# Attention loop of an adaLN network: exponential in two halves, paired table stores, one copy of the operands, a new order of the loads

## The chip, the cores and the metric

One core of a Trainium2 chip runs the whole kernel. The metric is the device time of one execution in microseconds, median of several; lower is better. Five engines with queues of their own work side by side and synchronise by semaphores: TensorE (PE, its weight loads shown as PEld), VectorE (DVE), ScalarE (ACT), GpSimd (POOL) and SyncE (SP), which here issues the DMAs.

## The reference, cut to what matters

The network has two layers; the change is in the attention of the first. That attention has relative positions, 16 heads of 16 channels, 8 sequences of 1024 tokens:

```python
Q = _heads(x @ Wq.T + bq)
K = _heads(x @ Wk.T + bk)
V = _heads(x @ Wv.T + bv)
rel = jnp.arange(t)[None, :] - jnp.arange(t)[:, None]
rel_pos = jnp.clip(rel + ATT_SPAN, 0, 2 * ATT_SPAN - 1)      # ATT_SPAN = 128
scores = jnp.einsum('bhqd,bhkd->bhqk', Q, K) * scale
c2p = jnp.einsum('bhqd,shd->bhqs', Q, pos_key) * scale
c2p = jnp.take_along_axis(c2p, rel_pos[None, None, :, :], axis=-1)
p2c = jnp.einsum('bhkd,shd->bhks', K, pos_query) * scale
p2c = jnp.take_along_axis(p2c, p2c_pos[None, None, :, :], axis=-1)
scores = scores + c2p + jnp.swapaxes(p2c, -1, -2)
probs = jax.nn.softmax(scores, axis=-1)
ctx = jnp.einsum('bhqk,bhkd->bhqd', probs, V)
```

Before it stand a layer norm with modulation and the projections; behind it an output projection, a quantised feed-forward layer, a second layer with a state-space scan and one more feed-forward layer. The change touches none of these.

## The kernel before, in words

`attention_loop` goes over 128 heads (8 sequences by 16), two to a turn of its loop (`pair`), and in each head over 8 query tiles of 128 rows, `i` = 0 to 7. `m` counts tiles over all heads, `n` counts heads.

The position terms differ from key to key only within 128 positions. For every tile two **tables** of 128 by 384 are computed (queries against relative keys, `e` even, and keys against relative queries, `e` odd), 16 to a head, one head ahead. PE multiplies them into `e_ps` (`table`, L883), ACT copies each to `tab` (`keep_table`, L966), SP stores it to DRAM (`store_table`, L784), and SP reads it back **skewed**, with a row pitch one element shorter, so that relative positions become key positions (`load_skew`, L793). The skewed reads go in four parts of two tiles (`PARTS`), each of four DMAs. A part's reads wait until its tables' stores have landed.

For query tile m the stages are: PE **scores** (L866, bf16 products of operands in `opnd`) plus transposed additions of the skewed key table (L870), DVE **add** of the skewed query table (L1018) and negated row **maximum** (L1020), ACT **exponential** over all 1024 keys (L971), PE **turn**: eight transposes of the probabilities (L899) in two halves of 512 keys, a copy of each half to `probsT` (first half DVE L1025; second half DVE L1028 in even tiles, ACT `keep_second` L978 in odd ones), and PE **context** (L918). Every fourth tile adds `keep_context` (ACT L985), `sum_lanes` (PE L928) and `normalise` (DVE L1036, L1039).

Each engine runs its work in the written order; iteration i (tile m) is:

- PE: scores(m+1), table 2i, turn(m), table 2i+1, at i = 1 and 5 sum_lanes, context(m-1).
- ACT: keep_table 2i, keep_table 2i+1, exps(m+1), at odd i keep_second(m), at i = 0 and 4 keep_context.
- DVE: add and maximum of m+1, copies of turn(m), at i = 1 and 5 normalise.
- SP, at the head's start: the three operand loads of head n+1 (`load_opnd`, L771), two loads of a second operand copy for the tables of head n+2 (`load_eopnd`, L775; the same first 96 rows of the same DRAM arrays). Then in iteration i the stores of tables 2i and 2i+1; behind those of i = 0 the skewed reads of part 3 (tiles 6 and 7 of head n) and the load of the values; behind i = 2, 4 and 6 the skewed reads of parts 0, 1 and 2 of head n+1.

Waits that bind the engines to each other: scores(m+1) needs exps(m-1) done (two score buffers). The scores of tiles 0, 1, 3 and 5 also wait for the skewed reads of parts 0, 1, 2 and 3. turn(m) needs exps(m), and each of its halves needs the copy of the same half of turn(m-1), since `pT_ps` has one buffer for each half. There is one `e_ps`, so table e+1 needs keep_table e done. These two lines carry most of what follows:

```python
ge(pe, s_exp, m + 1)        # turn, first half: the exponential of this tile
ge(pe, s_p1a, n * HALF + i // 2)   # turn, second half, even i: ACT's copy of the tile before
```

Of the kernel before, what the change touches and what calls it, by code (L numbers as in the profile page):

```python
# [15 lines left out]
P = 128  # L16
# [4 lines left out]
SPAN = 128  # L21
# [678 lines left out]
def attention_loop(nc, ident, key_ext, query_ext, q_st, kl_st, kr_st, v_st, table_dram, ctx_dram, heads, T):  # L700
# [7 lines left out]
    NEAR = 3 * P  # L708
    NE = 2 * TT
    PARTS = tuple((t, t + 2) for t in range(0, TT, 2))  # L710
    LAG = 3
    GROUP = BANK // P
    GROUPS = TT // GROUP
    LANES = P // VW
# [3 lines left out]
    with ExitStack() as ctx:  # L718
# [10 lines left out]
        eopnd = sb("eopnd", [ROWS, 2, 2, T], BF16)  # L729
# [12 lines left out]
        pT_ps = pb("pT_ps", [P, 2, BANK])  # L742
        c_ps = pb("c_ps", [P, BANK])

        s_op = [sem(f"opnd_loaded{u}") for u in range(2)]
        s_eop = [sem(f"eopnd_loaded{u}") for u in range(2)]
# [20 lines left out]
        @block.sync  # L767
        def _(sp):
            def load_opnd(n, u):
                for k, st in enumerate((q_st, kl_st, kr_st)):  # L770
                    sp.dma_start(opnd[:, u, k, :], st[bass.ds(n, 1), :, :].rearrange("a r t -> (a r) t")).then_inc(s_op[u], 16)  # L771

            def load_eopnd(n, u):
                for k, st in enumerate((q_st, kl_st)):
                    sp.dma_start(eopnd[:, u, k, :], st[bass.ds(n, 1), 0:ROWS, :].rearrange("a r t -> (a r) t")).then_inc(s_eop[u], 16)  # L775
# [5 lines left out]
            def store_table(n1, u1, e):  # L781
                ge(sp, s_tab, n1 * NE + e + 1)
                part = e // 2 // (TT // len(PARTS))
                sp.dma_start(table_dram[u1, e % 2, e // 2, 0:P, SPAN:SPAN + BAND], tab[:, e, :]).then_inc(s_tw[part], 16)  # L784

            def load_skew(n1, u1, part):
                a, z = PARTS[part]

                ge(sp, s_tw[part], n1 * (16 * 2 * (z - a)) + 16 * 2 * (z - a))
                for side, a1, z1, first, to, width in (  # L790
                        (0, a, z, 3 * P, P, 2 * P), (1, a, z, P - 1, 0, 2 * P),
                        (0, max(a, 1), z, P, 0, P), (1, a, min(z, TT - 1), 4 * P - 1, 2 * P, P)):
                    sp.dma_start(skew[:, u1, side, a1:z1, to:to + width],  # L793
                                 skewed(u1, side, a1, z1, first, width)).then_inc(s_sk[part], 16)

            def head(h):
                n, u = h.n, h.u
                ge(sp, s_add, n * TT)
                ge(sp, s_S, n * TT)
                load_opnd(n + 1, 1 - u)  # L800
                ge(sp, s_E, (n + 1) * NE)
                load_eopnd(n + 2, u)
                for i in range(TT):
                    for e in range(2 * i, 2 * i + 2):
                        store_table(n + 1, 1 - u, e)
                    for part, (_, z) in enumerate(PARTS):
                        if z - 1 + LAG - 1 == i + 1:
                            load_skew(n + 1, 1 - u, part)
                        if z - 1 + LAG - 1 == i + 1 + TT:
                            load_skew(n, u, part)  # L810
                    if i == 0:
# [7 lines left out]
            load_eopnd(0, 0)  # L819
            load_opnd(0, 0)  # L820
            load_eopnd(1, 1)
            load_val(0, 0)
            for e in range(NE):
                store_table(0, 0, e)
            for part in range(len(PARTS) - 1):
                load_skew(0, 0, part)
            def pair(j):
                for u in range(2):
                    head(Tile(j, u))
            pair(0)  # L830
            if heads // 2 > 1:
                with sp.Fori(1, heads // 2) as j:
                    pair(j)
            ge(sp, s_out, heads * GROUPS)
            sp.dma_start(ctx_dram[heads], out[:, 1, :]).then_inc(s_ctx[1], 16)
            for u in range(2):
                ge(sp, s_ctx[u], 16 * (heads // 2))

            ge(sp, s_op[0], 48 * (heads // 2 + 1))
            ge(sp, s_val[0], 16 * (heads // 2 + 1))  # L840
            for u in range(2):
                ge(sp, s_eop[u], 32 * (heads // 2 + 1))
            for part in range(len(PARTS)):
                ge(sp, s_sk[part], 64 * (heads + (part < len(PARTS) - 1)))

        @block.tensor
        def _(pe):
            def scores(m1, i, h):

                q, b, u = slice(i * P, (i + 1) * P), i % 2, h.u  # L850
                if i == 0:
                    ge(pe, s_op[u], h.j * 48 + 48)
# [4 lines left out]
                ge(pe, s_exp, m1 - 1)  # L857
# [17 lines left out]
            def table(h, e):  # L875

                n1, u1 = h.n, h.u
                if e == 0:
                    ge(pe, s_eop[u1], h.j * 32 + 32)
                ge(pe, s_tab, n1 * NE + e)  # L880
                side, t = e % 2, e // 2
                ext = (key_ext, query_ext)[side]
                mm = nc.tensor.matmul(e_ps[:, 0:BAND], eopnd[:, u1, side, t * P:(t + 1) * P],  # L883
                                      ext[:, bass.ds(n1 % HEADS, 1), :].rearrange("r a u -> r (a u)"),
                                      start=True, stop=True)
# [74 lines left out]
        def _(act):  # L960
            def keep_table(n1, e):
                act.wait_ge(s_E, n1 * NE + e + 1)
                part = [e < 2 * z for _, z in PARTS].index(True)

                ge(act, s_tw[part], n1 * (16 * 2 * (PARTS[part][1] - PARTS[part][0])))
# [1351 lines left out]
```

## Time and profile before

| | |
|---|---|
| median of 3 runs | 10667.31 us (10664.95 to 10668.15) |
| the profiled execution | 10648.76 us, span 10647.0 us |
| busy over the span | PE 79%, DVE 82%, ACT 51%, POOL 48% |
| exponentials L971 | 1025, mean 1114 ns |
| table copies L966 | 2064, mean 491 ns |
| transposes L899 | 8192, mean 279 ns |
| table stores | 2064 of 192 KB |

The profiled execution lies 18.5 us below the median. The shares are over the whole program; the attention loop is one stretch of it, from about 650 to 4045 us, in which POOL does nothing. The chain of the work that ended last covers only the last feed-forward layer, so it says nothing on this loop. "Mean ns" of matmuls is latency, since they are pipelined. A number in square brackets in the timeline is the idle time of that engine before the row, with what ended it.

### The profile page before, as it was taken

How to read it: one execution, taken by the hardware profiler on the slowest of the kernel's cores; microseconds unless marked ns; L12 is line 12 of the kernel's file. 1: busy time of each engine (PE TensorE's matmuls, PEld its weight loads, DVE VectorE, ACT ScalarE, POOL GpSimd, SP SyncE). 2: the span in 40 equal slices, each digit the busy share in tenths (PEclk: the TensorE clock that was granted, in tenths of full speed). 3: DMA queues.
4: the chain of work that ended last, by engine and by line, in shares of the span. 5: the costliest groups of instructions: out<-in, count | busy, mean ns of one | idle time of the engine just before them, and what ended most of it. 6: DMA issues, size and time to landing. Idle time of an engine off the chain costs nothing. (4 is left out here: it accounts for less than half of the span.)

```text
span 10647.0 us, 176766 instructions
## 1 busy us (share of the span) xinstructions
PE 8403.4 (79%) x48140; PEld 4814.3 (45%) x48140; DVE 8755.2 (82%) x13441; ACT 5475.6 (51%) x8829; POOL 5097.6 (48%) x4660
## 2 busy tenths in 40 slices
PE   4569999898999995797777777776677777777499
PEld 2246666666666664563333333322233333333266
DVE  4558888888888886896988888889688888888799
ACT  1247777777777772333544445444445554445233
POOL 0000000000000000684888888888688888888587
PEclk7789999999999997898898888888898888888799
DMA  5578888888888885111111111111211222122111
GB/s 178 204 240 279 281 282 281 280 280 278 281 281 281 279 278 166 50 43 68 71 49 61 73 65 49 68 73 39 84 72 54 77 81 81 45 76 81 41 43 40
DMA packets 1218156, 1498.79 MB, mean 141 GB/s; under 512 B 101997, under 2 KB 1073277, under 8 KB 1185000
## 3 DMA queue, kind: packets, MB, share of 16 engines
q1 hardware_dynamic: 1217832, 1495.78, 42.8%
q14 instruction: 280, 2.29, 0.1%
q8 instruction: 44, 0.72, 0.0%
HBM read 932.33 MB, written 564.60 MB: 141 GB/s over the span
## 5 line engine op out<-in xcount | busy, mean ns | idle before, releaser
L2156 PE MATMUL mb_y_ps<-mb_g,ident 128*128 128x512 f32 x4096 | 2285.9, 672 | 738.6 <-DVE mb_g L1957 475.9
L1898 POOL TENSOR_TENSOR mb_bx<-mb_dtu,mb_bc 128x512 f32<-128x512 f32 x2048 | 2638.2, 1314 | 221.1 <-DVE mb_hs L2007 186.2
L2188 ACT ACTIVATE mb_dA<-mb_dt,mb_a_neg 128x512 f32<-128x512 f32 x2048 | 1407.6, 690 | 2420.7 <-DVE mb_hs L2007 1486.2
L1355 POOL MEMSET f_magic<- 128x1 f32 x2 | 0.2, 99 | 3817.8 <-POOLq L127 3817.8
L2156 PEld LDWEIGHTS mb_y_ps<-mb_g,ident 128*128 128x128 f32 x4096 | 812.0, 212 | 1978.3 <-DVE mb_g L1957 764.6
L966 ACT ACTIVATE at_tab<-at_e_ps 128x384 f32<-128x384 f32 x2064 | 1013.6, 491 | 945.7 <-PE at_e_ps L883 944.6
L1020 DVE TENSOR_REDUCE at_nmax<-at_s_ps 128x1 f32<-128x1024 f32 x1025 | 1255.0, 1224 | 35.2
L899 PE MATMUL at_pT_ps<-ident,at_probs 128*128 128x128 f32 x8192 | 1110.6, 279 | 138.5 <-ACT at_probs L971 127.8
L971 ACT ACTIVATE at_probs<-at_s_ps,at_nmax 128x1024 f32<-128x1024 f32 x1025 | 1141.6, 1114 | 91.7 <-DVE at_nmax L1020 71.9
L1905 POOL TENSOR_TENSOR mb_g<-mb_hs_sb,mb_bc 128x512 f32<-128x512 f32 x704 | 903.5, 1283 | 464.3 <-DVE mb_hs_sb L2007 355.4
L899 PEld LDWEIGHTS at_pT_ps<-ident,at_probs 128*128 128x128 f32 x8192 | 912.9, 141 | 407.4 <-ACT at_probs L971 383.2
L2007 DVE TENSOR_TENSOR_SCAN mb_hs<-mb_dA,mb_carry,mb_bx 128x512 f32<-128x512 f32 x672 | 847.3, 1282 | 199.2 <-POOL mb_bx L1898 89.2
L1957 DVE TENSOR_TENSOR mb_g<-mb_hs,mb_bc 128x512 f32<-128x512 f32 x1344 | 906.6, 675 | 120.2 <-PE mb_y_ps L2156 119.9
L866 PE MATMUL at_s_ps<-at_opnd 105*128 105x512 bf16 (+3 forms) x2818 | 807.7, 327 | 190.7 <-DMA at_skew<-at_tables 189.2
L2007 DVE TENSOR_TENSOR_SCAN mb_hs<-mb_dA,mb_bx 128x512 f32<-128x512 f32 x672 | 815.5, 1224 | 153.2 <-POOL mb_bx L1898 67.1
L1018 DVE TENSOR_TENSOR at_s_ps<-at_s_ps,at_skew 128x384 f32<-128x384 f32 (+1 forms) x1025 | 540.6, 527 | 472.3 <-PE at_s_ps L870 354.8
L2090 PE MATMUL mb_ring<-mb_xc,mb_diag 128*128 128x512 f32 x1024 | 560.5, 634 | 177.6 <-ACT mb_u L2239 177.6
L1025 DVE COPY at_probsT<-at_pT_ps 128x512 f32<-128x512 f32 x1024 | 695.5, 679 | 0.0
L918 PE MATMUL at_c_ps<-at_probsT,at_val 128*32 128x128 f32 x16384 | 661.1, 279 | 1.6 <-ACT at_probsT L978 1.6
L870 PE MATMUL at_s_ps<-ident,at_skew 128*128 128x128 f32 x2818 | 611.5, 275 | 0.0
L918 PEld LDWEIGHTS at_c_ps<-at_probsT,at_val 128*32 128x32 f32 x16384 | 385.7, 109 | 212.5 <-issue 202.1
L2007 DVE TENSOR_TENSOR_SCAN mb_hs_sb<-mb_dA,mb_carry,mb_bx 128x512 f32<-128x512 f32 x352 | 447.4, 1271 | 12.2 <-DVE mb_v L1993 5.0
(229 smaller groups left out, 14436.9 us busy)
## 6 DMA issues: line engine op xcount, KB each, us to landing
at_tables<-at_tab SPq DMA_DIRECT2D x2064, 192.0 KB, 3.4
at_skew<-at_tables SPq DMA_DIRECT2D x1030, 256.0 KB, 3.0
mb_bc<-mb_bc_rows SPq DMA_DIRECT2D x256, 1024.0 KB, 6.6
at_skew<-at_tables SPq DMA_DIRECT2D x773, 128.0 KB, 3.4
at_opnd<-at_q_st SPq DMA_DIRECT2D x129, 210.0 KB, 3.4
at_opnd<-at_kl_st SPq DMA_DIRECT2D x129, 210.0 KB, 3.8
at_opnd<-at_kr_st SPq DMA_DIRECT2D x129, 210.0 KB, 5.0
at_eopnd<-at_q_st SPq DMA_DIRECT2D x130, 192.0 KB, 4.2
```

Source lines behind the costliest of these rows:

```text
L866: mm = nc.tensor.matmul(s_ps[:, b, a * P:z * P], opnd[:, u, 0, q], opnd[:, u, side, a * P:z * P], start=True, stop=(len(near) == 0))
L899: mm = nc.tensor.transpose(pT_ps[:, hb, k * P:(k + 1) * P], probs[:, i % 2, c:c + P], ident[:, :])
L918: mm = nc.tensor.matmul(c_ps[lane * VW:(lane + 1) * VW, q:q + P], val[:, h.u, k + lane, :], probsT[:, i0 % 2, (k + lane) * P:(k + lane + 1 ...
L966: nc.scalar.activation(tab[:, e, :], e_ps[:, 0:BAND], ACT.Copy).then_inc(s_tab, 1)
L971: nc.scalar.activation(probs[:, i % 2, :], s_ps[:, i % 2, :], ACT.Exp, bias=nmax[:, i % 2:i % 2 + 1], scale=1.0).then_inc(s_exp, 1)
L1020: nc.vector.tensor_reduce(nmax[:, b:b + 1], s_ps[:, b, :], axis=AX.X, op=ALU.max, negate=True).then_inc(s_max, 1)
L1898: pool.tensor_tensor(bx[:, s % RINGS, :], dtu[:, c, :], bc[:, 0, n, :], ALU.mult).then_inc(s_bx, 1)
L1905: pool.tensor_tensor(g[:, s1 % RINGS, :], state(s1), bc[:, 1, s1 % STATE, :], ALU.mult).then_inc(s_gp, 1)
L1957: nc.vector.tensor_tensor(g[:, s1 % RINGS, :], state(s1), bc[:, 1, n, :], ALU.mult).then_inc(s_g, 1)
L2007: nc.vector.tensor_tensor_scan(state(s), dA[:, s % DA_RING, :], bx[:, s % RINGS, :], initial=carry[:, s:s + 1] if k.u else 0.0, op0=ALU.mu ...
L2156: nc.tensor.matmul(y_ps[:, c % 2, :], ident[:, :], g[:, s1 % RINGS, :], start=(n == 0), stop=(n == STATE - 1)).then_inc(s_y, 1)
L2188: nc.scalar.activation(dA[:, s % DA_RING, :], dt[:, c, :], ACT.Exp, scale=a_neg[:, c, n:n + 1]).then_inc(s_dA, 1)
```

## The change

- The exponential of a tile is two instructions of 512 keys, each of which raises `s_exp`; the first half of the turn waits for the first, the second half for the second. Scores(m+1) wait for both halves of tile m-1.
- Two tables of a tile are stored by one DMA of 384 KB in place of two of 192 KB; it waits for both copies.
- `eopnd` and its two loads a head (192 KB each) are gone; the tables read the first 96 rows of `opnd`. The three operand loads of head n+2 are issued in iteration 6 of head n, after the scores of its last tile, each with a semaphore of its own.
- The skewed reads still go in four parts of two tiles, and at the same places among the table stores as before. Values are loaded in iteration 2 in place of 0.

```diff
+                if i == TT - 2:
+                    ge(sp, s_S, n * TT + TT)
+                    load_opnd(n + 2, u)
+                store_tables(n + 1, 1 - u, i)
+                if i == 2:
                     ge(sp, s_pv, n * TT)
                     load_val(n + 1, 1 - u)
...
-                if e == 0:
-                    ge(pe, s_eop[u1], h.j * 32 + 32)
+                if e < 2:
+                    ge(pe, s_op[e][u1], h.j * 16 + 16)
...
             def turn(m, i, n):
                 for hb in range(2):
+                    ge(pe, s_exp, m * 2 + 1 + hb)
                     if hb == 0:
-                        ge(pe, s_exp, m + 1)
                         ge(pe, s_p0, m)
...
-                nc.scalar.activation(probs[:, i % 2, :], s_ps[:, i % 2, :], ACT.Exp, bias=nmax[:, i % 2:i % 2 + 1],
-                                     scale=1.0).then_inc(s_exp, 1)
+                for hb in range(2):
+                    half = slice(hb * HC, (hb + 1) * HC)
+                    nc.scalar.activation(probs[:, i % 2, half], s_ps[:, i % 2, half], ACT.Exp, bias=nmax[:, i % 2:i % 2 + 1],
+                                         scale=1.0).then_inc(s_exp, 1)
```

**SP, before, around the boundary between two heads** (the last two table stores of head n's loop body, the operand loads, the stores of tables 0 and 1, the skewed reads of part 3, the values):

```order
L784 DMA at_tables<-at_tab 128x384 [waits at_table_kept] x2
L771 DMA at_opnd<-at_q_st 105x1024 [waits at_scores,at_near_added]
L771 DMA at_opnd<-at_kl_st 105x1024
L771 DMA at_opnd<-at_kr_st 105x1024
L775 DMA at_eopnd<-at_q_st 96x1024 [waits at_table_done]
L775 DMA at_eopnd<-at_kl_st 96x1024
L784 DMA at_tables<-at_tab 128x384 [waits at_table_kept] x2
L793 DMA at_skew<-at_tables 128x2x256 [waits at_table_stored3]
L793 DMA at_skew<-at_tables 128x2x256
L793 DMA at_skew<-at_tables 128x2x128
L793 DMA at_skew<-at_tables 128x128
L778 DMA at_val<-at_v_st 128x256 [waits at_context]
```

**SP, changed, the same place** (store of iteration 7, store of iteration 0, the skewed reads of part 3, stores of 1 and 2, values, contexts):

```order
L778 DMA at_tables<-at_tab 128x2x384 [waits at_table_kept]
L778 DMA at_tables<-at_tab 128x2x384 [waits at_table_kept,at_scores,at_near_added]
L788 DMA at_skew<-at_tables 128x2x256 [waits at_table_stored3]
L788 DMA at_skew<-at_tables 128x2x256
L788 DMA at_skew<-at_tables 128x2x128
L788 DMA at_skew<-at_tables 128x128
L778 DMA at_tables<-at_tab 128x2x384 [waits at_table_kept] x2
L772 DMA at_val<-at_v_st 128x256 [waits at_context]
L810 DMA at_ctx<-at_out 128x128 [waits at_out]
```

The five operand loads that stood ahead of the store of iteration 0 and of the reads of part 3 are gone from there, and the values stand two stores later.

**SP, changed, iterations 5 to 7** (where the three operand loads now are):

```order
L778 DMA at_tables<-at_tab 128x2x384 [waits at_table_kept]
L768 DMA at_opnd<-at_q_st 105x1024 [waits at_scores]
L768 DMA at_opnd<-at_kl_st 105x1024
L768 DMA at_opnd<-at_kr_st 105x1024
L778 DMA at_tables<-at_tab 128x2x384 [waits at_table_kept]
L788 DMA at_skew<-at_tables 128x2x256 [waits at_table_stored2]
L788 DMA at_skew<-at_tables 128x2x256
L788 DMA at_skew<-at_tables 128x2x128 x2
```

They stand ahead of the store of iteration 6 and the reads of part 2.

**ACT, before, iterations 3 and 4** (table copies of 3, exponential of tile 4, second-half copy of tile 3, table copies of 4, exponential of tile 5, context copy):

```order
L971 ACTIVATE at_probs<-at_s_ps,at_nmax 128x1024 [waits at_turned,at_max]
L966 ACTIVATE at_tab<-at_e_ps 128x384 [waits at_table_stored1,at_table_done] x2
L971 ACTIVATE at_probs<-at_s_ps,at_nmax 128x1024 [waits at_turned,at_max]
L978 ACTIVATE at_probsT<-at_pT_ps 128x512 [waits at_turned,at_context]
L966 ACTIVATE at_tab<-at_e_ps 128x384 [waits at_table_stored2,at_table_done] x2
L971 ACTIVATE at_probs<-at_s_ps,at_nmax 128x1024 [waits at_turned,at_max]
L985 ACTIVATE at_ctxT<-at_c_ps 128x512 [waits at_context_summed,at_context]
```

**ACT, changed, the same place:**

```order
L961 ACTIVATE at_tab<-at_e_ps 128x384 [waits at_table_stored1,at_table_done] x2
L968 ACTIVATE at_probs<-at_s_ps,at_nmax 128x512 [waits at_turned,at_max]
L968 ACTIVATE at_probs<-at_s_ps,at_nmax 128x512
L975 ACTIVATE at_probsT<-at_pT_ps 128x512 [waits at_turned,at_context]
L961 ACTIVATE at_tab<-at_e_ps 128x384 [waits at_table_stored2,at_table_done] x2
L968 ACTIVATE at_probs<-at_s_ps,at_nmax 128x512 [waits at_turned,at_max]
L968 ACTIVATE at_probs<-at_s_ps,at_nmax 128x512
L982 ACTIVATE at_ctxT<-at_c_ps 128x512 [waits at_context]
```

Nothing is reordered; the second-half copy and the two table copies of iteration 4 stand behind two exponentials in place of one.

## Rows read from the trace of the kernel before

**Rows 1.** Stretch: us, busy PE, PEld, DVE, ACT, POOL, clock, DMA share, GB/s.

```profile
2000.00:2100.00 100.00, 91.32 (x1032) 66.94 (x1031) 83.04 (x124) 72.58 (x115) 0.00 (x0) 1.00 0.89 278
```

**Rows 2.** Waits, 1500 to 3500 us: total us, times, longest; 76 heads.

```profile
PEld at_pT_ps L899 <- ACT at_probs L971: 228.7, 378, 0.8
...
PE at_s_ps L866 <- DMA at_skew<-at_tables: 105.4, 77, 2.3
PE at_pT_ps L899 <- ACT at_probs L971: 77.0, 245, 0.3
```

**Rows 3.** Timeline: start us, us, instruction, idle before and its releaser.

```profile
2016.90 0.34 PE L866 MATMUL at_s_ps<-at_opnd 105*128 105x384 bf16 x1
...
2017.85 1.04 PE L899 MATMUL at_pT_ps<-ident,at_probs 128*128 128x128 f32 x8
...
2019.56 0.39 PE L866 MATMUL at_s_ps<-at_opnd 105*128 105x512 bf16 x1
...
2019.83 1.11 ACT L971 ACTIVATE at_probs<-at_s_ps,at_nmax 128x1024 f32<-128x1024 f32 x1 [0.25 <-DVE at_nmax L1020]
...
2020.34 0.33 PE L883 MATMUL at_e_ps<-att_key_ext,at_eopnd 96*128 x1
...
2020.99 1.09 PE L899 MATMUL at_pT_ps<-ident,at_probs 128*128 128x128 f32 x8 [0.33 <-ACT at_probs L971]
2021.42 1.23 DVE L1020 TENSOR_REDUCE at_nmax<-at_s_ps 128x1 f32<-128x1024 f32 x1
...
2021.92 0.33 PE L883 MATMUL at_e_ps<-att_query_ext,at_eopnd 96*128 x1
...
2022.29 0.49 ACT L966 ACTIVATE at_tab<-at_e_ps 128x384 f32<-128x384 f32 x1 [0.96 <-PE at_e_ps L883]
...
2022.76 1.11 ACT L971 ACTIVATE at_probs<-at_s_ps,at_nmax 128x1024 f32<-128x1024 f32 x1
2023.77 0.59 ACT L978 ACTIVATE at_probsT<-at_pT_ps 128x512 f32<-128x512 f32 x1
...
2024.27 0.45 PE L866 MATMUL at_s_ps<-at_opnd 105*128 105x512 bf16 x2 [1.44 <-DMA at_skew<-at_tables]
...
2026.09 0.33 PE L883 MATMUL at_e_ps<-att_query_ext,at_eopnd 96*128 x1
...
2026.93 0.50 PE L866 MATMUL at_s_ps<-at_opnd 105*128 105x512 bf16 x2
```

**Rows 4.** Timeline of SP alone, which issues the DMAs.

```profile
2014.16 0.36 SPq L771 DMA_DIRECT2D at_opnd<-at_q_st  x1
...
2016.68 0.83 SPq L784 DMA_DIRECT2D at_tables<-at_tab  x2
2017.56 2.53 SPq L793 DMA_DIRECT2D at_skew<-at_tables  x4
```

**Rows 5.** DMA issues, 1500 to 3500 us: count, KB each, median us to landing.

```profile
at_tables<-at_tab SPq DMA_DIRECT2D x1216, 192.0 KB, 3.4
at_skew<-at_tables SPq DMA_DIRECT2D x606, 256.0 KB, 3.0
...
at_opnd<-at_q_st SPq DMA_DIRECT2D x76, 210.0 KB, 3.3
...
at_eopnd<-at_q_st SPq DMA_DIRECT2D x76, 192.0 KB, 4.2
```

**Rows 6.** Groups by shape, 1500 to 3500 us: busy us, mean ns, idle before.

```profile
L971 ACT ACTIVATE at_probs<-at_s_ps,at_nmax 128x1024 f32<-128x1024 f32 x607 | 676.0, 1114 | 50.8 <-DVE at_nmax L1020 38.9
```

**Rows 7.** The same view of ScalarE alone, 0 to 640 us.

```profile
L685 ACT ACTIVATE st_full<-st_qk_ps,st_bias 128x512 f32<-128x512 f32 x64 | 44.0, 687 | 91.8 <-PE st_qk_ps L640 91.8
```

**Rows 8.** Busy time by stretch, columns as in the first group.

```profile
2013.00:2025.00 12.00, 10.12 (x117) 7.49 (x110) 9.20 (x15) 8.71 (x14) 0.00 (x0) 1.00 1.02 333
2037.00:2039.00 2.00, 2.00 (x20) 1.40 (x21) 1.28 (x2) 1.47 (x4) 0.00 (x0) 1.00 0.35 109
```

**Rows 9.** Landing times of the operand loads, last line of their tile view.

```profile
DMA to landing us min/median/max: 2.9/3.8/6.0
```

More of the change, by code:

```diff
@@ L710, in attention_loop @@
     PARTS = tuple((t, t + 2) for t in range(0, TT, 2))
-    LAG = 3
     GROUP = BANK // P
@@ L728, in attention_loop @@
         opnd = sb("opnd", [OPND, 2, 3, T], BF16)
-        eopnd = sb("eopnd", [ROWS, 2, 2, T], BF16)
         tab = sb("tab", [P, NE, BAND])
@@ L743, in attention_loop @@
         c_ps = pb("c_ps", [P, BANK])
-        s_op = [sem(f"opnd_loaded{u}") for u in range(2)]
-        s_eop = [sem(f"eopnd_loaded{u}") for u in range(2)]
+        s_op = [[sem(f"{n}_loaded{u}") for u in range(2)] for n in ("q", "kl", "kr")]
         s_val = [sem(f"val_loaded{u}") for u in range(2)]
@@ L770, in load_opnd @@
                 for k, st in enumerate((q_st, kl_st, kr_st)):
[L771 to L775, printed above, removed]
+                    sp.dma_start(opnd[:, u, k, :],
+                                 st[bass.ds(n, 1), :, :].rearrange("a r t -> (a r) t")).then_inc(s_op[k][u], 16)
             def load_val(n, u):
@@ L779, in load_val, with store_tables @@
                              v_st[bass.ds(n, 1), :, :].rearrange("a p n -> (a p) n")).then_inc(s_val[u], 16)
[L781 to L784, printed above, removed]
+            def store_tables(n1, u1, t):
+                ge(sp, s_tab, n1 * NE + 2 * t + 2)
+                part = [t < z for _, z in PARTS].index(True)
+                sp.dma_start(table_dram[u1, :, t, 0:P, SPAN:SPAN + BAND].rearrange("s p u -> p s u"),
+                             tab[:, 2 * t:2 * t + 2, :]).then_inc(s_tw[part], 16)
             def load_skew(n1, u1, part):
                 a, z = PARTS[part]
-                ge(sp, s_tw[part], n1 * (16 * 2 * (z - a)) + 16 * 2 * (z - a))
+                ge(sp, s_tw[part], n1 * (16 * (z - a)) + 16 * (z - a))
                 for side, a1, z1, first, to, width in (
@@ L799, in head @@
                 ge(sp, s_S, n * TT)
-                load_opnd(n + 1, 1 - u)
-                ge(sp, s_E, (n + 1) * NE)
-                load_eopnd(n + 2, u)
                 for i in range(TT):
-                    for e in range(2 * i, 2 * i + 2):
-                        store_table(n + 1, 1 - u, e)
                     for part, (_, z) in enumerate(PARTS):
-                        if z - 1 + LAG - 1 == i + 1:
+                        if z + 1 == i:
                             load_skew(n + 1, 1 - u, part)
-                        if z - 1 + LAG - 1 == i + 1 + TT:
+                        if z + 1 == i + TT:
                             load_skew(n, u, part)
-                    if i == 0:
+                    if i == TT - 2:
[3 more added lines that the diff above has]
+                    if i == 2:
                         ge(sp, s_pv, n * TT)
@@ L817, in head @@
                                      out[:, 1 - u, :]).then_inc(s_ctx[1 - u], 16)
-            load_eopnd(0, 0)
-            load_opnd(0, 0)
-            load_eopnd(1, 1)
+            for u in range(2):
+                load_opnd(u, u)
             load_val(0, 0)
-            for e in range(NE):
-                store_table(0, 0, e)
+            for t in range(TT):
+                store_tables(0, 0, t)
             for part in range(len(PARTS) - 1):
@@ L837, in _ @@
                 ge(sp, s_ctx[u], 16 * (heads // 2))
-            ge(sp, s_op[0], 48 * (heads // 2 + 1))
+            for k in range(3):
+                for u in range(2):
+                    ge(sp, s_op[k][u], 16 * (heads // 2 + 1))
             ge(sp, s_val[0], 16 * (heads // 2 + 1))
-            for u in range(2):
-                ge(sp, s_eop[u], 32 * (heads // 2 + 1))
+            for part, (a, z) in enumerate(PARTS):
+                ge(sp, s_tw[part], 16 * (z - a) * (heads + 1))
             for part in range(len(PARTS)):
@@ L851, in scores @@
                 if i == 0:
-                    ge(pe, s_op[u], h.j * 48 + 48)
+                    ge(pe, s_op[2][u], h.j * 16 + 16)
                     ge(pe, s_sk[0], h.n * 64 + 64)
@@ L856, in scores @@
                         ge(pe, s_sk[part], h.n * 64 + 64)
-                ge(pe, s_exp, m1 - 1)
+                ge(pe, s_exp, m1 * 2 - 2)
                 lo, hi = max(0, i - 1), min(TT, i + 2)
@@ L882, in table @@
                 ext = (key_ext, query_ext)[side]
-                mm = nc.tensor.matmul(e_ps[:, 0:BAND], eopnd[:, u1, side, t * P:(t + 1) * P],
+                mm = nc.tensor.matmul(e_ps[:, 0:BAND], opnd[0:ROWS, u1, side, t * P:(t + 1) * P],
                                       ext[:, bass.ds(n1 % HEADS, 1), :].rearrange("r a u -> r (a u)"),
@@ L963, in keep_table @@
                 part = [e < 2 * z for _, z in PARTS].index(True)
-                ge(act, s_tw[part], n1 * (16 * 2 * (PARTS[part][1] - PARTS[part][0])))
+                ge(act, s_tw[part], n1 * (16 * (PARTS[part][1] - PARTS[part][0])))
                 nc.scalar.activation(tab[:, e, :], e_ps[:, 0:BAND], ACT.Copy).then_inc(s_tab, 1)
```

## The prediction, made before the changed kernel ran

> **What bounds the kernel now.** The view by stretches comes first [rows 1]: in the steady attention loop PE is busy 91% of the time, DVE 83%, ACT 73%, and the DMA engines 89% at 278 GB/s. No engine is full, so the loop is bound by a circle of waits. The groups give its period: 607 exponentials in 2000 us [rows 6] are 3.295 us a tile and 26.36 us a head; 128 heads are 3374 us of the 10649.
>
> The waits view says what PE, the busiest, waits for [rows 2]. PE's scores wait for skewed reads 77 times in 76 heads, 105.4 us together: once a head, 1.39 us. Its turns wait for the exponential, 77.0 us on PE and 228.7 us on the weight loads, so between 1.0 and 3.0 us a head.
>
> The timeline shows both [rows 3]. Iteration 2 starts with its scores at 2016.90, turns at 2017.85, 0.95 later, and gives way to iteration 3 at 2019.56: 2.66 us with no wait. In iteration 3 the turn comes at 2020.99, 1.43 after the scores: it waited 0.48 us for the exponential that ran from 2019.83 to 2020.94. Then the scores of tile 5 wait 1.44 us, to 2024.27, for the reads of part 3. Iteration 4 takes 2.66 us again (to 2026.93).
>
> Why are those reads late? SP issued them from 2017.56 to 2020.09 [rows 4]. Ahead of them stood, from 2014.16 to 2016.68, three operand loads and two second-copy loads: 3 x 210 + 2 x 192 = 1014 KB [rows 5]. The DMA engines were full from 2013 to 2025, share 1.02 at 333 GB/s, while two iterations later the share falls to 0.35 [rows 8]. So there is no lack of bandwidth over the head, but a crowd at its start.
>
> **The change part by part.**
>
> *Loads moved and dropped.* The two second-copy loads are gone and the three operand loads stand in iteration 6. Ahead of the reads of part 3 SP thus issues 2.5 us less, and the DMA has 1014 KB less to move: 1.04 MB at 333 GB/s is 3.1 us. The lateness was 1.44 us, so either alone covers it. I count this wait as gone. Its worth is not the full 1.39, since iteration 4 began late enough for its exponential to be waiting ready. Without the wait, iteration 4 would start at 24.27 - 1.44 = 2022.83 and its turn would be due at 2023.78, while the exponential of tile 4 runs from 2022.76 to 2023.87 whatever PE does (it follows the maximum, 2021.42 to 2022.65). The turn then starts at 2023.92, 0.14 late; its table, 0.93 after it as in iteration 3 (2020.99 to 2021.92), is multiplied at 2024.85 in place of 2026.09 [rows 3]. So: **-1.24 us a head**.
>
> *The exponential in halves.* A pointer-bias activation of 128x512 out of PSUM takes 687 ns [rows 7], against 1114 ns for 1024 columns [rows 6]. Successive ACT instructions overlap by 0.10 (2022.76 + 1.11 against 2023.77 [rows 3]). With start E the first half is ready at E+0.69, the second at E+1.28, and ACT goes on at E+1.18 in place of E+1.01: 0.17 us more ACT time a tile. ACT has room for it in sum: 72.6% of 26.36 is 19.1 us a head, and 8 x 0.17 makes 20.5.
>
> The half turn can start 0.42 us sooner, which is what the 0.48 us waits of the odd iterations need. But what is next? Take iteration 4 with the change. Iteration 3's turn no longer waits, so PE arrives about 0.43 sooner. The exponential of tile 4 hardly moves: it follows the maximum (DVE, end 2022.65), so E = 2022.70. First half ready 2023.39: the first half turn is off. The second half of the turn needs ACT's copy of the same half of tile 3, which stands behind both exponentials: it starts at 22.70 + 1.18 = 2023.88 and ends 0.59 later, at 2024.47. The table copy behind it ends at about 2024.86 and frees `e_ps`, so the second table is multiplied at 2024.91. Without halves it was 2024.85. **The wait of PE goes from the exponential in the odd iteration to ACT's copies in the even one, and +0.06 us remains.** That happens after tiles 3 and 7. After tiles 1 and 5 PE has the lane sums to do first (about 0.9 us), which cover ACT; in those iterations the wait lost (about 0.3 to 0.5) is matched by one for the table copy behind `keep_context`. So +0.12 us a head; I take 2 x 0.06. Bounds: at best all turn waits go and nothing comes in their place (-3.0, the whole of the weight loads' waits), at worst all ACT time is on the path (+1.4). I choose near zero because the walk on the rows gives that, but both bounds stay for the range.
>
> The Trainium skill (ScalarE: Activation LUTs, What ACT_TABLE_LOAD costs) gives 280 ns + 0.833 ns a column with a pointer bias and an overlap of 93 ns. That speaks against this edit: 707 ns a half, 0.19 us more ACT time a tile in place of 0.17, and the sum would differ by hundredths. The trace agrees with it within 20 ns at both widths.
>
> *Paired stores.* 8 fewer issues a head free SP of about 3 us (two stores take it 0.83 [rows 4]). SP computes nothing; its time matters only for when reads leave. The even table leaves one table copy later (about 1 us), and the stores were at 3.4 us to landing [rows 5]; the reads wait for stores of the iteration before last, so I count nothing. If the pair lands 1 us later, part reads leave up to 1 us later: slack is 2.66 x 3 = 8.0 us from store to scores, less 2.5 of issue and 4.2 of landing (2020.09 to 2024.27), 1.3 us.
>
> *384 KB less a head.* 5% of the traffic. No wait is for bandwidth once the crowd is gone: nothing.
>
> *Operand loads in iteration 6.* New wait: SP waits for the scores of tile 7, and the stores of iteration 6 and the reads of part 2 are queued behind. These scores end 0.8 us into iteration 6 and the tables of that iteration are kept only at its end, so the stores aren't held. The new reader is the first table of iteration 0, two iterations and 0.78 us (2019.56 to 2020.34 [rows 3]) after iteration 6 starts: 2.66 x 2 + 0.78 - 0.8 = 5.3 us. The query operand lands 3.3 us after issue [rows 5], worst case of the three 6.0 [rows 9]. Nothing, with 2 us to spare at the median.
>
> **Sum:** -1.24 + 0.12 = -1.12 us a head, x 128 = -143 us. 10649 - 143 = 10506 for an execution like the profiled one; the median lies 18.5 us above that, so 10524. New period 25.2 us.
>
> **The rivals.**
>
> *R1, the halves pay.* If ACT is not late in the even iterations (the exponential starts earlier than I think, because DVE too gets its turned halves sooner), half of the 4 x 0.48 = 1.9 us of turn waits comes back: -1.24 - 0.95 = -2.2 us a head, -280 us, 10387. For: ACT has 20% idle, DVE's 83% are 21.9 us, so 24.2 is possible. Against: maximum and copies on DVE set E, and no edit touches them.
>
> *R2, another read is late.* Part 2's reads stand behind 630 KB of operands (1.9 us at 333 GB/s) with 1.3 us of slack at the worst landing. If 0.7 us a head comes back: -0.4 x 128 = -54, 10613. Against: DMA share there is 0.35.
>
> *R3, slower.* The operands of head n+2 come too late for its first table. It costs PE one for one, and everything behind. It decides from 5.3 + 1.12 = 6.4 us between issue and landing; at 7.4 it is 1.0 us a head slower than before, +123 us, 10790. For: a wait that formerly had a whole head of slack. Against: 6.0 was the longest landing, in the crowd.
>
> *R4, nothing moves.* The skewed reads are late for another reason, the store they wait for; 10667 within 20.
>
> **How the numbers follow.** Forecast 0.55, R1 0.25, R2 0.10, R3 0.04, R4 0.06. Leaving out R3 and R4 the range goes from R1, 10387, to R2, 10613: 10390 to 10615. About 0.2%, 21 us, is what a measurement of this kernel can tell from no change. Faster: 0.90. Same: 0.06. Slower: 0.04.
>
> **What would show it.** In the profile after: PE's wait for skewed reads falls from 1.39 us a head to under 0.2; no new wait for operands (R3) or for part 2 (R2); the 128x512 exponentials take 0.69; the wait of turns for the exponential shrinks, while the second turn half and the second table wait for ACT's copies, mostly in iterations 4 and 0; DMA still near 278 GB/s, since 5% fewer bytes go in 4% less time. If the latter waits are missing and the period is under 24.6 us, R1 holds. What makes me wrong most easily is E: if the maximum comes earlier, the whole walk of ACT shifts.

## The result, and the profile after

The changed kernel takes 10483.78 us, median of 4 runs (10480.07 to 10492.34), against 10666.13 us for the kernel before on the same chip: a ratio of 0.9831, 95% interval 0.9814 to 0.9849. The forecast was 10524 in a range of 10390 to 10615; the saving is 182 us where 143 was forecast. Of the two profiled executions (10648.76 and 10492.34) the difference is 156 us: the one before lies 17 us under its median of 10666.13, the one after 9 us over its own.

Executions of the kernel before differ from chip to chip by up to 25 us (medians 10645 to 10670). So below the times are compared as ratios to the kernel before on the same chip, and the traces by the period of the loop (us a head). Where an expectation names a time in us, it was reckoned from the 10667 and 10484 measured for the two kernels at first.

The groups by shape of the changed kernel, 1500 to 3500 us (busy us, mean ns, idle before):

```profile
L968 ACT ACTIVATE at_probs<-at_s_ps,at_nmax 128x512 f32<-128x512 f32 x1270 | 802.4, 684 | 48.3 <-DVE at_nmax L1017 34.9
L1017 DVE TENSOR_REDUCE at_nmax<-at_s_ps 128x1 f32<-128x1024 f32 x635 | 777.6, 1225 | 21.7
```

635 tiles stand in the window where there were 607 [rows 6]: 2000 / 635 x 8 = **25.20 us a head**, against 26.36. That is the forecast 25.2. It is 1.16 us a head less, 148 us over 128 heads, so nearly all of the 156 us lies in this loop. A half exponential takes 684 ns, as the 687 of [rows 7] said.

Waits of the same window (total us, times, longest), then SP's own:

```profile
ACT at_tab L961 <- PE at_e_ps L878: 359.6, 716, 0.6
...
PE at_pT_ps L894 <- ACT at_probsT L975: 57.8, 142, 0.5
```
```profile
SPq L778 <- ACT at_tab L961: 392.5, 300, 2.6
SPq L788 <- DMA at_tables<-at_tab: 380.4, 281, 3.6
SPq L768 <- PE at_s_ps L865: 42.4, 63, 1.1
```

Against [rows 2]: PE's wait for skewed reads, 105.4 us, has no row any more, nor has PE's wait for the exponential, 77.0 us. In their place PE's turn waits 57.8 us for ScalarE's copy `at_probsT`, a wait that has no row in the kernel before. And SP, which waited for ScalarE only 78.5 us in the kernel before, waits for it 392.5 us here:

```profile
SPq L793 <- DMA at_tables<-at_tab: 458.4, 227, 3.7
SPq L784 <- ACT at_tab L966: 78.5, 273, 0.6
```

(that is SP before, same window). A store waits here for the table that ScalarE has yet to copy, so this wait tells that SP is early; when it is missing, SP is late.

The timeline of iteration 4 after the change, which begins at 2012.40 (start us, us):

```profile
2012.61 1.26 ACT L968 ACTIVATE at_probs<-at_s_ps,at_nmax 128x512 f32<-128x512 f32 x2 [0.19 <-DVE at_nmax L1017]
...
2013.35 0.66 PE L894 MATMUL at_pT_ps<-ident,at_probs 128*128 128x128 f32 x4
...
2013.77 0.60 ACT L975 ACTIVATE at_probsT<-at_pT_ps 128x512 f32<-128x512 f32 x1
2013.99 1.22 DVE L1017 TENSOR_REDUCE at_nmax<-at_s_ps 128x1 f32<-128x1024 f32 x1
2014.24 0.50 ACT L961 ACTIVATE at_tab<-at_e_ps 128x384 f32<-128x384 f32 x1
2014.51 0.63 PE L894 MATMUL at_pT_ps<-ident,at_probs 128*128 128x128 f32 x4 [0.50 <-ACT at_probsT L975]
2014.97 0.33 PE L878 MATMUL at_e_ps<-att_query_ext,at_opnd 96*128 x1
```

The first half of the turn runs at 2013.35, 0.74 after the exponential began. The second half waits 0.50 us, not for its exponential (ready at 2013.87) but for ScalarE's copy of the same half of the tile before, which stands behind both exponentials and ends at 2014.37. This is the mechanism of the prediction's walk: from the start of the exponential to the end of that copy it had 1.77 us, and 1.76 passed.

The DMA line of the same window for both kernels, before first:

```profile
DMA packets 551140, 560.70 MB, mean 280 GB/s; under 512 B 47058, under 2 KB 512608, under 8 KB 551140
```
```profile
DMA packets 548920, 555.56 MB, mean 278 GB/s; under 512 B 36571, under 2 KB 524035, under 8 KB 548920
```

560.70 / 607 x 8 is 7.39 MB a head, 555.56 / 635 x 8 is 7.00 MB. The rate hardly changed, as forecast. (A rate is these bytes divided by the period, so it carries nothing that the two don't.)

### The profile page after: what moved, and what is told of

The parts are those of the page before. It is cut to its first block and busy times, and to the rows that moved or that the text cites. A ratio compares the mean times of both kernels' runs of the same rounds, so it can differ in the third digit from the quotient of the medians.

```text
span 10490.6 us, 176903 instructions
## 1 busy us (share of the span) xinstructions
PE 8462.0 (81%) x48140; PEld 4814.2 (46%) x48140; DVE 8771.6 (84%) x13441; ACT 5600.9 (53%) x9854; POOL 5093.0 (49%) x4660
## 5 line engine op out<-in xcount | busy, mean ns | idle before, releaser
L968 ACT ACTIVATE at_probs<-at_s_ps,at_nmax 128x512 f32<-128x512 f32 x2050 | 1295.2, 684 | 84.9 <-DVE at_nmax L1017 63.2
L894 PE MATMUL at_pT_ps<-ident,at_probs 128*128 128x128 f32 x8192 | 1189.9, 278 | 95.7 <-ACT at_probsT L975 94.9
```

The source lines that it names most:

```text
L894: mm = nc.tensor.transpose(pT_ps[:, hb, k * P:(k + 1) * P], probs[:, i % 2, c:c + P], ident[:, :])
L968: nc.scalar.activation(probs[:, i % 2, half], s_ps[:, i % 2, half], ACT.Exp, bias=nmax[:, i % 2:i % 2 + 1], scale=1.0).then_inc(s_exp, 1)
```

## The experiments

My theory at the start was: the gain is the wait for the part-3 reads, removed because the operand loads no longer stand ahead of them; the bytes and the paired stores are worth nothing; the halves shift one wait into another. The halves and the pairing were run alone and left out; the loads were moved in the kernel before, but the second copy was never dropped by itself.

### The halves alone, and the change without them

`halves_only` is the kernel before with this edit and PE's waits for the two halves; `no_halves` undoes both in the changed kernel. (`...` stands for arguments that both lines share.)

```diff
-                nc.scalar.activation(probs[:, i % 2, :], s_ps[:, i % 2, :], ACT.Exp, ...).then_inc(s_exp, 1)
+                for hb in range(2):
+                    half = slice(hb * HC, (hb + 1) * HC)
+                    nc.scalar.activation(probs[:, i % 2, half], s_ps[:, i % 2, half], ACT.Exp, ...).then_inc(s_exp, 1)
```

> The kernel before with the exponential in two halves and nothing else of the change. Theory (the gain is the wait for the part-3 reads; the halves only shift PE's wait to ScalarE's copies): within 20 us of before, 10650 to 10685; PE's wait for skewed reads stays near 1.4 us a head or grows. Rival (the halves bring it): 10480 to 10560.

Measured: 10636.88 us, ratio 0.9995 (0.9986 to 1.0004), period 26.36 us (607 tiles), the same as before. The time lies under the expected range only because this chip's kernel before stands at 10645. PE's wait for skewed reads fell from 105.4 to 83.5 us where it was expected to stay or grow; at 16 of these places PE's scores wait for the exponential instead, 21.6 us.

> The changed kernel with the exponential in one piece again; loads, shared operands and paired stores stay. Theory: 10465 to 10500, about 15 us under or level with the changed kernel (10484), no wait for skewed reads, PE's turns wait for the exponential again. Rival (the halves bring it): 10600 or more.

Measured: 10441.57 us, ratio 0.9811 (0.9798 to 0.9825), period 2000 / 644 x 8 = 24.84 us:

```profile
L1015 DVE TENSOR_REDUCE at_nmax<-at_s_ps 128x1 f32<-128x1024 f32 x644 | 788.5, 1224 | 22.1
```
```profile
PE at_pT_ps L894 <- ACT at_probs L966: 51.3, 161, 0.3
```

So the whole gain, and somewhat more, comes from the other parts: 1.52 us a head. The halves cost 25.20 - 24.84 = 0.36 us a head, 46 us over 128 heads where about 15 was expected. The intervals of the ratios of the changed kernel and `no_halves` overlap, so by their times alone this loss is not settled; by the period it is plain, and `single_stores` below, which has the changed kernel's period and ran on the chip of `no_halves`, took 51 us more than it. Without the halves PE waits for the exponential again, 51.3 us, less than the 57.8 that it waits for the copy with them.

Where in a head the time goes is seen best iteration by iteration: the mean distance, in us, from the first scores of an iteration (those of tile i+1) to those of the next, in the traces from 1500 to 3500 us, 71 to 81 heads each. The last three kernels are explained further down.

| iteration | 0 | 1 | 2 | 3 | 4 | 5 | 6 | 7 |
|---|---|---|---|---|---|---|---|---|
| before | 2.85 | 3.84 | 2.66 | **4.66** | 2.72 | 3.99 | 2.55 | 3.11 |
| `no_halves` | 2.90 | 3.80 | 2.66 | 3.20 | 2.98 | 3.69 | 2.55 | 3.08 |
| changed | 3.19 | 3.76 | 2.66 | 2.99 | **3.40** | 3.76 | 2.55 | 2.87 |
| `order_only` | **3.57** | 3.83 | 2.66 | 3.22 | 2.97 | 3.70 | 2.59 | **5.68** |
| `spread` | 2.75 | 3.95 | 2.66 | 3.20 | 2.98 | 3.70 | **3.74** | 3.30 |
| `second_first` | 3.16 | 3.81 | 2.66 | 2.99 | 2.88 | 3.93 | 2.55 | 2.87 |

Iteration 3 ends with the scores of tile 5, which wait for part 3. It falls from 4.66 to 3.20 without the halves: that is the gain.

### Is it the place of the loads?

`order_only` is the kernel before with its five loads moved behind the part-3 reads.

```diff
-                load_opnd(n + 1, 1 - u)
-                ge(sp, s_E, (n + 1) * NE)
-                load_eopnd(n + 2, u)
                 for i in range(TT):
...
                             load_skew(n, u, part)
                     if i == 0:
+                        load_opnd(n + 1, 1 - u)
+                        ge(sp, s_E, (n + 1) * NE)
+                        load_eopnd(n + 2, u)
                         ge(sp, s_pv, n * TT)
```

> The kernel before with its five operand loads of the head's start moved behind the part-3 reads of iteration 0; same bytes, same number of DMAs, two copies, whole exponential. Theory (what counts is what stands ahead of the reads): 10485 to 10530, the wait for skewed reads gone. Rival (fewer bytes are what counts): 10600 to 10667.

Measured: 10873.25 us, ratio **1.0212** (1.0198 to 1.0226), period 28.22 us (567 tiles). Both expectations fail as to the time. What the trace shows (waits, then PE's wait in the timeline, then SP around it):

```profile
PE at_s_ps L866 <- DMA at_skew<-at_tables: 184.6, 77, 3.8
```
```profile
SPq L793 <- DMA at_tables<-at_tab: 593.8, 284, 3.7
SPq L784 <- ACT at_tab L966: 46.5, 156, 0.5
```
```profile
2016.24 0.23 PE L866 MATMUL at_s_ps<-at_opnd 105*128 105x128 bf16 x1 [1.83 <-DMA at_skew<-at_tables]
```
```profile
2007.81 1.87 SPq L784 DMA_DIRECT2D at_tables<-at_tab  x4
2010.91 1.92 SPq L793 DMA_DIRECT2D at_skew<-at_tables  x4
2012.94 2.08 SPq L784 DMA_DIRECT2D at_tables<-at_tab  x4
2017.10 1.92 SPq L793 DMA_DIRECT2D at_skew<-at_tables  x4
```

The part-3 reads are on time now (iteration 3 takes 3.22), as the theory said, but those of part 1 are late: they are due at the scores of tile 1, where iteration 7 ends, and it takes 5.68. SP never waits long for ScalarE (46.5 us in 71 heads), yet it waits 593.8 us for stores to land: it is late all through the head. It issues four stores in 1.9 us, waits 1.2 us (to 2010.91) or 2.1 us (to 2017.10) until one of them has landed, issues four reads in 1.9 us, and so on. When SP is on time the same wait is shorter, since the store in question left an iteration earlier: in `single_stores` below, whose stores are as many, it is 206 us. In the kernel before the five loads stood between a store and the reads that wait for it, and filled that wait; moved behind the reads they fill nothing, and SP falls further behind. I read this as: **SP's serial chain of issues and landings had no time to spare in the kernel before**; the row of 78.5 us against 392.5 above agrees.

`spread` therefore puts the loads where SP would wait anyway, in two places, with all bytes kept:

```diff
                 for i in range(TT):
+                    if i == 2:
+                        ge(sp, s_E, (n + 1) * NE)
+                        load_eopnd(n + 2, u)
+                    if i == 4:
+                        load_opnd(n + 1, 1 - u)
```

> The kernel before, with the two second-copy loads at the start of iteration 2 and the three operand loads at the start of iteration 4, each ahead of that iteration's stores, so that they are issued while SP would wait for a store to land. Same bytes, same DMA count, whole exponential. Theory (place and SP's own serial chain decide, not bytes): a ratio near that of no_halves, 0.981 to 0.987; the wait for skewed reads under 0.3 us a head. Rival (384 KB less a head is what counts): 0.995 or more.

Measured: 10631.24 us, ratio 0.9976 (0.9966 to 0.9987), period 26.27 us (609 tiles). By the period these two places are worth 0.1 us a head of 1.52, and the rival's range holds. But the wait for part 3 is gone here too, with all the bytes kept: iteration 3 takes 3.20, as in `no_halves`. New waits ate the gain, at the scores of tile 0 (the end of iteration 6, 3.74 in place of 2.55), which need the operands just loaded, and at those of tile 1 (the end of iteration 7), which need part 1:

```profile
PE at_s_ps L868 <- DMA at_opnd<-at_kr_st: 70.7, 61, 2.6
...
PE at_s_ps L868 <- DMA at_skew<-at_tables: 43.6, 64, 1.9
```
```profile
DMA packets 552966, 562.65 MB, mean 281 GB/s; under 512 B 47231, under 2 KB 514368, under 8 KB 552966
```

SP issues the first operand load 16.85 us (median) after iteration 0 begins, although iteration 4 begins after 12.6: it is 4.3 us late. The changed kernel issues it after 20.75 us, 1.0 into iteration 6. So the place of the loads decides which transfer is late, not only whether one is. The place that the change itself chose, iteration 6 and two heads ahead, was not tried with the second copy kept.

### Is it SP's issue time?

`single_stores` takes the pairing out of the changed kernel; `pairs_only` puts it alone into the kernel before (its diff follows; the counts that others wait for change with it).

```diff
-            def store_table(n1, u1, e):
-                ge(sp, s_tab, n1 * NE + e + 1)
-                part = e // 2 // (TT // len(PARTS))
-                sp.dma_start(table_dram[u1, e % 2, e // 2, 0:P, SPAN:SPAN + BAND], tab[:, e, :]).then_inc(s_tw[part], 16)
+            def store_tables(n1, u1, t):
+                ge(sp, s_tab, n1 * NE + 2 * t + 2)
+                part = [t < z for _, z in PARTS].index(True)
+                sp.dma_start(table_dram[u1, :, t, 0:P, SPAN:SPAN + BAND].rearrange("s p u -> p s u"),
+                             tab[:, 2 * t:2 * t + 2, :]).then_inc(s_tw[part], 16)
```

> The changed kernel with two stores of 192 KB a tile in place of one of 384 KB. Theory (SP's issue time is hidden): within 15 us of the changed kernel, 10470 to 10500. Rival (the issue time or the landing of pairs matters): over 10510, or under 10460.

Measured: 10492.99 us, ratio 0.9858 (0.9843 to 0.9873), period 25.20 us (635 tiles), that of the changed kernel.

```profile
SPq L779 <- ACT at_tab L961: 289.6, 532, 1.2
SPq L788 <- DMA at_tables<-at_tab: 206.1, 210, 2.5
```

SP still waits 289.6 us for ScalarE, so it has time for the eight more issues, as the first theory expected. (The ratio looks worse than the changed kernel's, 0.9831; the medians, 10493 and 10484 on different chips, and the equal periods show no loss.)

> The kernel before with two tables stored by one DMA and nothing else of the change: the five loads stay at the head's start. New theory (SP's own serial chain of issues and waits for landings sets the period of the kernel before; it waited for ScalarE only 1.0 us a head): 8 issues of 0.4 us fewer a head are worth 1 to 3 us a head until the engines bind at about 24.9, ratio 0.981 to 0.990. Rival (the crowd of the DMA engines behind the head's start makes the part-3 reads late, whatever SP does): within 0.3% of before.

Measured: 10603.64 us, ratio 0.9963 (0.9949 to 0.9976), period 26.10 us (613 tiles). Faster, beyond the rival's 0.3%, but 0.26 us a head and not 1 to 3. The issue time that was saved came back as waiting for landings:

```profile
SPq L794 <- DMA at_tables<-at_tab: 731.5, 283, 4.7
SPq L784 <- ACT at_tab L966: 36.3, 120, 1.2
```
```profile
DMA packets 546787, 566.42 MB, mean 283 GB/s; under 512 B 37753, under 2 KB 507748, under 8 KB 546787
```

458.4 us of such waits were in the kernel before. A store now lands 4.4 us after its issue at the median, in place of 3.4. So SP is late, but its issue time is at most a small part of what makes it late.

### What is left: the bytes

Four kernels with 384 KB more a head than the changed one, and three SP programs between them, have nearly the same period and rate: before 26.36 us at 280 GB/s, `halves_only` 26.36 at 280, `spread` 26.27 at 281, `pairs_only` 26.10 at 283. Two more kernels of this kind follow below. In all of them SP waits for ScalarE under 80 us of the 2000. `no_halves`, without the 384 KB, takes 24.84 us at 282 GB/s. That these rates are equal proves nothing: `order_only` has the bytes of the kernel before and 263 GB/s, and in `no_halves` SP waits 319.5 us for ScalarE, so it isn't SP and the DMA that stop that kernel at 282.

Fewer bytes is what I had as the rival in `order_only` and `spread` and had counted at nothing in the prediction. What the runs show is that no placement tried with the second copy came under 26.1 us, and that SP had time to spare in every kernel without it. Whether its 384 KB, its two DMA issues or the new place of the other three loads does it stays open: the loads of the second copy were never left out with all else kept.

The rate of 280 is not that of full DMA engines, which moved 333 GB/s in the crowded stretch [rows 8]. In these kernels a head's traffic goes stores, landing, reads, stores, and I take it that it runs dry while SP waits; no run shows this apart.

### ScalarE's copy ahead of the exponential

The new wait of the turn can be removed by giving ScalarE's second-half copy an earlier place. It needs only the turn before it, which PE has finished by then.

```diff
                         keep_table(n + 1, 2 * i)
+                        if i % 2 == 1:
+                            keep_second(m, i, n)
                         keep_table(n + 1, 2 * i + 1)
                         exps(m + 1, (i + 1) % TT)
-                        if i % 2 == 1:
-                            keep_second(m, i, n)
```

> The changed kernel with ScalarE's second-half copy of odd tiles ahead of the second table copy and the exponential, in place of behind the exponential. Theory (in even iterations the second turn half and the second table wait for copies that stand behind both exponentials, 0.54 us in iteration 0 and 0.74 in iteration 4): those waits go, 0.1 to 0.15 us come back in odd iterations: -0.9 us a head, 10350 to 10400. Rival (the period is held by VectorE or PE, and these waits only take up slack): 10465 to 10490.

Measured: 10442.23 us, ratio 0.9789 (0.9776 to 0.9803), period 24.81 us (645 tiles). The wait is gone, and 0.39 us a head with it, where 0.9 was expected. The gain is in iteration 4 (3.40 to 2.88); iteration 0, where 0.54 was expected, still takes 3.16, and iteration 5 grew by 0.17. In iteration 0 PE and its weight loads now wait for operands that land late:

```profile
PE at_e_ps L878 <- DMA at_opnd<-at_q_st: 17.4, 31, 1.3
```
```profile
SPq L788 <- DMA at_tables<-at_tab: 614.8, 317, 4.3
SPq L778 <- ACT at_tab L961: 170.9, 258, 1.8
```
```profile
DMA packets 557125, 564.07 MB, mean 282 GB/s; under 512 B 37113, under 2 KB 531610, under 8 KB 557125
```

SP's reserve fell from 392.5 to 170.9 us and landings take 614.8 us of its waiting. The 17.4 us are 0.2 us a head; the rest of the missing 0.5 was not traced.

> The same reordering on the changed kernel with the exponential in one piece. Theory (halves pay only once ScalarE's copies are out of the way): slower than second_first by 60 to 150 us, 10430 to 10500, with the turns of odd iterations waiting for the exponential. Rival (halves never pay): equal to second_first within 15 us.

Measured: 10476.97 us, ratio 0.9821 (0.9807 to 0.9834), period 25.12 us (637 tiles). The turns wait for the exponential, 93.8 us. It is 35 us slower than `second_first`, between the theory's 60 and the rival's 15. So the sign of the halves depends on where the copy stands: behind the exponentials they cost 0.36 us a head, ahead of them they bring 25.12 - 24.81 = 0.31. But the move by itself costs 25.12 - 24.84 = 0.28 against `no_halves`, so the two together only reach the period that the kernel had with neither: 24.81 against 24.84.

> second_first, and the context copy moved from behind the exponential of iterations 0 and 4 to between the two table copies of iterations 1 and 5. Theory (the second table of iterations 1 and 5 waits 0.23 us for a copy behind the context copy): -0.4 us a head against second_first, so 10300 to 10350. Rival (slack is taken elsewhere): within 10 us of second_first.

```diff
+                        if i % GROUP == 1 and not (isinstance(m, int) and m == 1):
+                            group = i // GROUP - 1
+                            keep_context(group % GROUPS, n if group >= 0 else n - 1)
```

(between the table copies, and the same removed behind the exponential at `i % GROUP == 0`; `keep_second` stands as in `second_first`.) Measured: 10441.96 us, ratio 0.9785 (0.9772 to 0.9798), period 24.84 us (644 tiles), the same as `second_first`; the rival holds. This and `second_first` have the lowest ratios of the study, but by the period `no_halves` is level with them.

### The slower case, and two attempts to lift the limit

`late_operands` moves the three operand loads behind the store of iteration 6:

```diff
+                    store_tables(n + 1, 1 - u, i)
                     if i == TT - 2:
                         ge(sp, s_S, n * TT + TT)
                         load_opnd(n + 2, u)
-                    store_tables(n + 1, 1 - u, i)
```

> The changed kernel with the three operand loads behind the store of iteration 6 in place of ahead of it, so about 2 us later. Theory (5.3 us stand between issue and first use, landing takes 4.6): the first table of the next head waits about 1.5 to 2.5 us a head, 10600 to 10800; this is the slower case of the prediction. Rival (the slack is larger): within 20 us of 10484.

Measured: 10573.72 us, ratio 0.9905 (0.989 to 0.9921), period 25.89 us (618 tiles).

```profile
PE at_e_ps L878 <- DMA at_opnd<-at_q_st: 60.8, 54, 2.1
```

60.8 us in 77 heads is 0.79 us a head, and the period grew by 0.69. The slower case exists, at less than half the price that was expected: the first operand load was issued 2.8 us later in the head (median) than in the changed kernel, but landed after 3.7 us, not 4.6. In the changed kernel the query operand lands 4.6 us after its issue, not 3.3, and three heads wait for it, 1.4 us together: the margin to 5.3 was thinner than forecast, and held.

`spread_best` combines `spread`, the halves and both early copies; `spread_best_pairs` adds the paired stores.

> spread with the exponential in halves and both copies of ScalarE early, as in both_first. Theory (both_first loses 0.3 us a head to operands that land after their first use; a second copy loaded long before has no such wait): 0.3 us a head better than both_first, ratio 0.975 to 0.978. Rival (traffic 5% higher makes reads late): 0.980 or more.

Measured: 10628.99 us, ratio 0.9968 (0.9956 to 0.998), period 26.32 us (608 tiles). The rival's range holds: with the second copy back, and the operand loads in iteration 4, the loop is as slow as before.

> spread_best with paired stores. New theory (spread_best was held at 26.28 us a head by SP, which waited for ScalarE only 0.5 us a head): SP gets 3 us a head back and the engines bind at 24.5 to 24.8, ratio 0.975 to 0.980. Rival (the operand loads are late at their place whatever SP does): over 0.990.

Measured: 10605.02 us, ratio 0.9964 (0.995 to 0.9977), period 26.10 us (613 tiles), that of `pairs_only`, although ScalarE's order and the place of the loads differ between the two; the rival's range holds again:

```profile
SPq L794 <- DMA at_tables<-at_tab: 760.4, 306, 4.7
SPq L784 <- ACT at_tab L968: 21.2, 73, 0.4
```
```profile
DMA packets 547140, 566.22 MB, mean 283 GB/s; under 512 B 37735, under 2 KB 508569, under 8 KB 547140
```

SP waits for ScalarE 21.2 us in 77 heads: ScalarE hardly ever holds SP up. ScalarE's new order, which brought 0.39 us a head in `second_first`, brought nothing in `spread_best`. So I take SP and the DMA to be what bounds the kernels with the second copy.

## Why the prediction was right, and where its steps were wrong

*The wait for skewed reads goes: right.* It was 105.4 us and has no row now. **Its term was mis-sized: -1.24 forecast, -1.52 measured** (26.36 to 24.84, `no_halves`). By the table, iteration 3 lost 1.46 and iteration 4 took 0.26 back, where the walk had 0.14 for a turn that would wait for its exponential. The walk left out iteration 5, which lost 0.30: PE's turn waited 0.3 us for its exponential there, a wait that `no_halves` doesn't have. As I read it, the late scores had also set back VectorE and ScalarE.

*Why it goes: right for this wait, wrong for the loop.* The prediction said that the loads' place made the part-3 reads late. `order_only` and `spread` bear that out: with the same bytes in another place, iteration 3 falls to 3.2. The step that failed is to take the loss of this wait for a gain of the loop: "so there is no lack of bandwidth over the head, but a crowd at its start". In both runs other transfers became late in its place, and the loop came to 28.22 and 26.27 us. That nothing else became late in the changed kernel is what the prediction gave no reason for; it counted the 384 KB less, the other half of that edit, at nothing. The idle stretch with a DMA share of 0.35 wasn't a reserve that SP could use. The view that would have warned was open: SP's own waits, 78.5 us for ScalarE in 76 heads, 458.4 us for landings.

*The halves: right in mechanism, mis-sized: +0.12 forecast, +0.36 measured.* The walk gave 2.84 us for iteration 3 (2019.56 to 2022.40, the 2022.83 of the walk less 0.43); measured it is 2.99, because the second half of that turn waited for the second half of its own exponential. In the timeline of the changed kernel the turn, which takes 1.04 where it doesn't wait, takes 1.30:

```profile
2009.69 1.26 ACT L968 ACTIVATE at_probs<-at_s_ps,at_nmax 128x512 f32<-128x512 f32 x2 [0.25 <-DVE at_nmax L1017]
...
2010.43 1.30 PE L894 MATMUL at_pT_ps<-ident,at_probs 128*128 128x128 f32 x8
```

For iteration 4 the walk gave 25.75 - 22.40 = 3.35, measured 3.40. So the two waits that the walk named are there. Against `no_halves` iterations 3 and 4 together lose 0.21 us and iterations 7 and 0 lose 0.08, where the walk had 0.06 for each pair; most of the difference is the wait that it skipped.

*Paired stores, no term: right in the changed kernel* (`single_stores`, equal period), *wrong for the kernel before* (`pairs_only`, -0.26 us a head). The same edit is worth something only where SP is late.

*Operands in iteration 6: right, with less to spare* than the 2 us claimed: 4.6 us to landing against 5.3.

The errors of -0.28 and +0.24 us a head nearly cancel, so that the period came out as forecast to the hundredth is luck. The loop accounts for 148 us and the two profiled executions differ by 156, both near the 143 forecast. The medians differ by 182 because the profiled executions lie 17 us under and 9 us over theirs; such differences have no row in the traces. (R2's sum is given as -0.4 x 128 = -54; that product is -51, and -54 belongs to the unrounded -0.42.)

*Rivals.* R1, the halves pay, is false as the kernel stands; with the copy moved they bring 0.31 us a head, but no more than that move costs without them. R2 did not occur. R3's wait was made to happen in `late_operands`, at 0.7 us a head, which still left it faster than the kernel before. R4 fell.

## What to carry to other kernels

Before crediting a late transfer to what stands ahead of it, look at what the issuing queue waits for: if it hardly ever waits for its data and often for landings, it is late all along, and another order of the same transfers moved the wait to the next deadline in `order_only` and `spread`. Compare a head iteration by iteration, since the period alone hid in `spread` that the wait aimed at was gone. Splitting an instruction so that its consumer starts sooner pays only if what stands behind it in its own queue isn't what that consumer needs next; moving that work ahead turned a loss of 0.36 us a head into a gain of 0.31, but the move had its own price of 0.28, so compare with the kernel that has neither edit. Dropping a private copy trades traffic for a deadline, so measure the landing time against it.

## What the runs showed of the hardware

Twelve of the fourteen kernels of this loop moved between 278 and 283 GB/s, and `late_operands` 270 and `order_only` 263, while a crowded stretch of the first reached 333 [rows 8]. And eight fewer DMA issues a head, some 3 us of SP's time, left the loop only 0.26 us a head faster: one store of 384 KB landed 4.4 us after its issue in `pairs_only` (3.8 in the changed kernel), one of 192 KB 3.4 us in the kernel before [rows 5].
